# Zeroed rows in the recurrence, a weight split in pieces and a shared chunk: one change to a two-layer recurrent kernel with expert gates

## The reference

```
xn = layernorm(x)
s  = recurrence(xn)                  # layer 0
f  = experts(xn)                     # layer 0
x  = x + s * silu(f)
xn = layernorm(x)
s  = scan(xn)                        # layer 1: a two-component oscillator per state, 64 states
f  = ffn(xn)                         # layer 1: w2(silu(w1 xn) * (w3 xn)), inner width 704, 8 weight sets
x  = x + s * silu(f)
```

```
x_lerp = h + delta * x_proj_mu                      # delta = previous position - h
x0 = tanh(x_lerp @ xl_w1.T) @ xl_w2.T + xl_b2       # 256 -> 32 -> 160
x2 = einsum(tanh(x0) as 5 x 32, x_out_w)            # 5 x 256 blend weights
r, k, v, g = (h + delta * mu_i) @ W_i.T
w  = tanh((h + delta * w_mu) @ w_w1.T) @ w_w2.T + w_b          # 256 -> 64 -> 128
o_t = r_t . S + sum(r_t * bonus * k_t) * v_t ;  S = S * exp(-exp(w_t)) + k_t v_t
out = (groupnorm(o) * weight + bias) * silu(g) @ o_w.T
```

## Time and profile before

| what | us |
|---|---|
| median of the runs | 5183.19 |
| lowest, highest of 3 runs | 5174.28, 5184.97 |
| the profiled execution, its own time | 5169.71 |
| span in its trace | 5168.1 |

### The profile page before, as it was taken

One profiled execution on the slowest core, in us unless ns is written; L12 is line 12 of the kernel. 1 busy time (PEld: TensorE's weight loads), 2 busy tenths in 40 slices (PEclk: granted clock), 3 DMA queues, 4 the chain that ended last, 5 costly groups with the idle time before them and its releaser, 6 DMA issues. The chain is left out here.

```text
span 5168.1 us, 80399 instructions
## 1 busy us (share of the span) xinstructions
PE 4565.2 (88%) x29148; PEld 3603.7 (70%) x29148; DVE 2719.6 (53%) x5127; ACT 1988.2 (38%) x3685; POOL 1665.3 (32%) x1322
## 2 busy tenths in 40 slices
PE   6605999999999999799999999999997798888885
PEld 6604988988989899466666666666665677777774
DVE  4484333333333343365555555555554477777775
ACT  2203454444444444143333333333333343434431
POOL 1103444434344443332322222322332223333333
PEclk9999999999999999788887888888887899999998
DMA  6622322223232222100000000000000434433432
GB/s 207 219 94 66 50 53 57 44 57 59 39 63 41 60 42 36 32 21 17 22 17 22 17 18 21 22 17 17 21 17 16 132 83 99 97 91 89 99 66 37
DMA packets 246853, 294.07 MB, mean 57 GB/s; under 512 B 19041, under 2 KB 223585, under 8 KB 242401
## 3 DMA queue, kind: packets, MB, share of 16 engines
q0 software_dynamic: 85760, 117.74, 13.3%
q1 hardware_dynamic: 135136, 137.74, 8.3%
q10 hardware_dynamic: 25600, 33.56, 1.9%
HBM read 154.62 MB, written 134.35 MB: 56 GB/s over the span
## 5 line engine op out<-in xcount | busy, mean ns | idle before, releaser
L578 DVE TENSOR_TENSOR e_hTl<-e_hf,e_hTh 128x512 fp32r<-128x512 f32 x512 | 355.0, 694 | 775.0 <-ACT e_hTh L521 774.9
L1031 POOL TENSOR_TENSOR a_mix<-a_tmp,a_h 128x512 f32<-128x512 f32 x320 | 384.1, 1217 | 993.0 <-DVE a_tmp L1090 845.7
L442 POOL DMA_INDIRECT acc_d<-e_y,e_sids x256 | 402.4, 1572 | 723.8 <-DVE e_y L594 678.9
L520 ACT ACTIVATE e_hf<-ps_heads,e_b 128x512 f32<-128x512 f32 x512 | 353.2, 690 | 645.0 <-PE ps_heads L665 641.7
L665 PE MATMUL ps<-e_w2h,e_hTh 128*128 128x256 f32 x2048 | 585.7, 286 | 0.0
L665 PE MATMUL ps<-e_w2h,e_hTl 128*128 128x256 f32 x2048 | 583.6, 285 | 0.0
L665 PE MATMUL ps<-e_w2l,e_hTh 128*128 128x256 f32 x2048 | 577.7, 282 | 0.0
L665 PE MATMUL ps_heads<-e_xTh,e_w1h 128*128 128x512 f32 x1024 | 419.6, 410 | 41.6 <-ACT e_hTh L521 28.9
L665 PE MATMUL ps_heads<-e_xTh,e_w1l 128*128 128x512 f32 x1024 | 408.7, 399 | 0.0
L665 PE MATMUL ps_heads<-e_xTl,e_w1h 128*128 128x512 f32 x1024 | 407.7, 398 | 0.0
L665 PEld LDWEIGHTS ps<-e_w2h,e_hTh 128*128 128x128 f32 x2048 | 392.9, 192 | 19.8
(11 more groups left out here) (287 smaller groups left out, 10089.4 us busy)
## 6 DMA issues: line engine op xcount, KB each, us to landing
r_x<-in_L_attn_hidden_states SPq DMA_DIRECT2D x32, 512.0 KB, 3.8
xn_d<-r_xn ACTq DMA_DIRECT2D x32, 512.0 KB, 3.1
xnT_d<-r_xT ACTq DMA_DIRECT2D x32, 512.0 KB, 3.4
acc_d<-r_zeros POOLq DMA_DIRECT2D x16, 1024.0 KB, 21.1
e_w<-in_L_ffn_w SPq DMA_DIRECT2D x16, 1024.0 KB, 4.9
s_d<-a_s SPq DMA_DIRECT2D x32, 512.0 KB, 2.9
f_a<-acc_d SPq DMA_DIRECT2D x32, 512.0 KB, 3.8
f_x<-s_d SPq DMA_DIRECT2D x32, 512.0 KB, 5.2
```

Source lines behind the costliest of these rows:

```text
L442: pool.indirect_dma_start(acc_d, bass.IndirectOffsetOnAxis(ap=sids[:, GT * q + t:GT * q + t + 1], axis=0), ys[r][:, t, :], None, compute_o ...
L520: nc.scalar.activation(hf[m % 2][:], ps[2 + m % 2][:], ACT.Gelu, bias=b1s[:, m:m + 1])
L578: nc.vector.tensor_tensor(hT[q % 2][1][:, m, :], hf[m % 2][:], hT[q % 2][0][:, m, :].bitcast(F32), ALU.subtract).then_inc(h_sb, 1)
L1031: nc.gpsimd.tensor_tensor(mix[n][:, m, :].rearrange("p (c t) -> p c t", c=GT), tmp[i % 2][:].rearrange("p (c t) -> p c t", c=GT), h[q % 2] ...
```

## The change

It has three parts, one for each of the three large stages.

**Recurrence.** The six operands with few rows (`w2`, `xot`, `dw2`, `low`, `x1t`, `dlow`) become tiles of 128 rows and are set to zero by POOL once; loads and tanh outputs fill the rows in use, and the matmuls take all 128 rows. The zeroes add nothing to the sums. The count of matmuls and of their columns stays. The loads of the three weights move behind the zeroing. The fifth and sixth entry of `AT` move one piece later, and the r product with what hangs on it becomes a piece of its own, issued at the start of slot `CHUNK` (7) ahead of the chunk; `FRONT` grows from 7 to 8.

```
-        low = sb("a_low", [RANK, GN])
+        low = sb("a_low", [P, GN])
-        x1t = sb("a_x1t", [RANK, GN])
+        x1t = sb("a_x1t", [P, GN])
-        dlow = sb("a_dlow", [GATE, GN])
+        dlow = sb("a_dlow", [P, GN])
...
-        FRONT = SLOTS - LATE
+        FRONT = SLOTS - LATE + 1
-        AT = {2: (0, 1), 3: (2, 3), 4: (4, 5), 5: (6, 7), 6: (8, 9)}
+        AT = {2: (0, 1), 3: (2, 3), 4: (4, 5), 6: (6, 7), 7: (8, 9)}
...
-                        piece(g + 1, f1[1], s - LATE, False)
+                        piece(g + 1, f1[1], s - LATE if s < CHUNK else s - LATE + 1, False)
                 for s in range(SLOTS):
                     if s < LEVELS:
                         level(g, r, s, first)
+                    if left and s == CHUNK:
+                        piece(g + 1, f1[1], CHUNK - LATE, False)
...
-            nc.gpsimd.memset(xo[:], 0.0).then_inc(set_up, 1)
+            for operand in (xo, w2, xot, dw2, low, x1t, dlow):
+                nc.gpsimd.memset(operand[:], 0.0).then_inc(set_up, 1)
...
-                    nc.scalar.activation(low[:], ready(LOW)[0:RANK, :], ACT.Tanh).then_inc(act_out, 1)
+                    nc.scalar.activation(low[0:RANK, :], ready(LOW)[0:RANK, :], ACT.Tanh).then_inc(act_out, 1)
```

```
+        W2_PARTS = 4
+        W2_AT = {1: 0, 2: 1, 4: 2, 5: 3}
...
-            def split_down(e):
+            def split_down(e, n):
+                if n == 0:
+                    act.wait_ge(y_sum, YS * e + 1)
                 act.wait_ge(down_in, 32 * e + 32)
-                nc.scalar.copy(w2p[0][:], w2s[:]).then_inc(w2_high, 1)
+                nc.scalar.copy(w2p[0][:, w2_part(n), :], w2s[:, w2_part(n), :]).then_inc(w2_high, 1)
...
-                split_down(e)
+                nc.scalar.activation(table[:], ident[:, 0:1], ACT.Gelu)
...
+                        if q == 0 and m in W2_AT:
+                            split_down(e, W2_AT[m])
...
-                    act.wait_ge(down_ps, DOWNS * (e + 1))
```

```
-        w1s = sb("f_w1", [P, KD, FF])
-        w3s = sb("f_w3", [P, KD, FF])
+        w1s = sb("f_w1", [P, KD, FC * P])
+        w3s = sb("f_w3", [P, KD, FF - REST])
...
                 for m in range(FC):
                     multiply(g, m)
+                    scans = (j, r) if q == QB - 1 else (j - 1, 1 - r) if not first or k >= QB else None
+                    if scans:
+                        scan_part(*scans, q, m, 0, 1)
+                    low_h(g, m)
+                    if m == 2 and not last:
+                        statistics(i, k + 1)
                     if m == 3:
                         if not first or k >= LAG:
                             gated(g - LAG, (k - LAG) % PAIR)
                         if not last:
-                            statistics(i, k + 1)
-                    if m == 4 and not last:
-                        centre(g + 1)
-                    if q == QB - 1:
-                        scan_part(j, r, q, m)
-                    elif not first or k >= QB:
-                        scan_part(j - 1, 1 - r, q, m)
-                    low_h(g, m)
+                            centre(g + 1)
+                    if scans:
+                        scan_part(*scans, q, m, 1, None)
...
-                    if m == 5 and not last:
+                    if m == 4 and not last:
                         normalise(i, k + 1)
...
+                    if bank == 4 and m == FC - 1:
+                        break
                     if not begin or m >= 2:
                         pe.wait_ge(free, n - 1)
+                    if bank == 2 and not begin and m == (FC - 1) % 2:
+
+                        pe.wait_ge(h_sb, n - 1)
...
+                    else:
+                        for n, v in enumerate(w2p):
+                            done = nc.tensor.matmul(to, hT[0][:, m, u * P:(u + 1) * P], v[:, m, :], start=False,
+                                                    stop=n == 1 and u % 2 == 1)
```

More of the change, by code:

```diff
@@ L40 @@
 FC = (FF + P - 1) // P
-def width(m):
-    return min(P, FF - m * P)
+REST = FF - (FC - 1) * P
 class Order:
@@ L354, in experts_phase @@
         yl = sb("e_yl", [B, D])
+        table = sb("e_table", [P, 1])
         up_in = sem("e_up_in")
@@ L1641, in _ @@
             pool.sem_inc(down_split, 1)
-            for part in w1p + w3p + w2p:
-                nc.gpsimd.memset(part[:].bitcast(F32), 0.0).then_inc(padded, 1)
+            nc.gpsimd.memset(w2p[1][0:REST, FC - 1, :].bitcast(F32), 0.0).then_inc(padded, 1)
             nc.gpsimd.memset(power[:], -0.5).then_inc(set_up, 1)
```

161 lines of the change are left out of this document (94 added, 67 removed).

## The result

| | us |
|---|---|
| before, median of 4 runs | 5178.73 (5167.5 to 5184.97) |
| changed, median of 4 runs | 4757.05 (4751.61 to 4764.4) |
| ratio | 0.9191, 95% interval 0.9179 to 0.9203 |
| profiled execution, its own time and span | 4756.55 and 4755.0 |

The account below looks back on a forecast made before the run. PE was taken to bound all three stages, with its clock in the recurrence and clock and waits elsewhere. 290 + 69 + 115 = 474 us off 5169.7 gave 4696, stated as 4700, range 4625 to 4810.

Parts of the forecast that it names:

- the two slow stretches: Recurrence: per group 13.6 and 6.8 us at half clock; widening the operands ahead removes both, 28 x 10.2 = 286 us.
- The 6 us that were given to the earlier r product: Recurrence: moving the r product earlier saves 6 of the 19.1 us PE waits for the copy of r.
- Rival 2: Recurrence: rows have nothing to do with the clock; some 20 us instead of 290, total 4970; 8 in 100.
- Rival 1: Recurrence: only one slow stretch per group goes, or falls come back elsewhere; total 4795 or 4890; 9 in 100.
- Rival 4: Recurrence: r product, pulled ahead, blocks PE in order; 4880 one slot late, 5240 three slots late; 2 in 100.
- The step on the left-over matmuls: Experts: cutting the run of 48 16-column matmuls in four removes the half clock behind it, 24 us.
- 19.3 - 12.9 = 6.4 us, 7 times: 45 us: Experts: an expert's first group shrinks from 19.3 us to ACT's 12.9 us, at seven starts, 45 us.
- The light tiles: Second layer: removed matmuls and the vanished wait for normalised rows take these tiles from 30.8 to 27.4 us.
- the tiles with scans: Second layer: shorter waits for the low part take the two heavy tiles from 38.8 and 38.6 to 35.5 and 33 us.
- DVE is idle a quarter of the tile now, part of it while ACT casts the weights, and that stays: Second layer, tiles with scans: reason for taking 35.5 and 33 us, above DVE's limit of some 30 and 28.
- a bound from below of 59 us: Second layer: lowest gain expected, from the removed matmuls alone, 32 x 1.83 = 59 us.
- Rival 3: Second layer: DVE bounds tiles with scans, new order only moves waits; 59 us gain, total 4756; 11 in 100.

Follow-up runs that it names:

- the fastest kernel: Changed kernel plus later load of the experts' first weight and the second layer's up weights split in two parts at the old place: 4723.03 us, ratio 0.9116.

## Why the prediction was right, and where it was off

The time lies in the range, 57 us above the middle. The recurrence carries the result and was right in its mechanism; the two other stages gave less than was forecast, and the reasons were not among the rivals.

**The recurrence: right in mechanism, and in size by two errors that cancel.** 290 us were forecast, 298 came by the trace. Counting half of the two slow stretches was nearly the right price: 286 counted, 270 in the stage for the rows alone, since the jumps back of the loop now cost PE waits and short falls of the clock. The 6 us that were given to the earlier r product were too few: on top of the rows the new order gives 28 us in the stage, of which some 19 are the waits for the copy of r. Taken one by one the two pairs of few-row operands give 205 and 102 us, 190 and 95 by the same count.

The Trainium skill ("TensorE: Matmul & The Clock Gate", section "LDWEIGHTS (loading the stationary operand)") says that a weight's load time does not depend on its rows, and the traces agree: a load of `a_xot` takes 184 ns on the mean with 32 rows and 189 with 128. What its Part 1 says of the clock, that it is set by how busy PE has been, does not cover this case: the stretches at 0.50 are those in which PE is 100% busy.

Rival 2 is out. Rival 1 is out for the whole change, but falls that come and go without a change of rows are what the order alone and a_x1t alone show. Rival 4's block of PE never came. A new wait of over 1 us on PE did come, in one group of four.

**The experts were forecast at 69 and gave 40.** The step on the left-over matmuls held: 24 forecast, 27.5 found, and no fall behind them. The step that failed is the start of an expert, "19.3 - 12.9 = 6.4 us, 7 times: 45 us", in two terms. The first is the count. The eighth expert stands behind the loop, without a jump, and its first group took 13.3 us before the change already; the 28.9 us of waits are six of 4.4 to 4.9 us and one of 0.5, not seven. Six times 6.4 is 38 us. The second is the wait ahead of the start. ACT and the casts went as reckoned, but the sum began at PE's first matmul: the unnamed wait of 2.02 us in the earlier trace rows was taken as fixed. With PE sooner at the jump, the fetch of its instructions met the 1 MB load, the wait grew by 2.2 us on the mean, and half clock around it kept the first group at 15.2 us on the mean instead of 12.9. So 19.7 - 15.2 - 2.2 = 2.3 us are left of each start, 14 us for six. With the load out of the way the stage takes 1591.5 us, 64 less than before, which is what six starts and the left-over rows make in the forecast's own prices (38 + 24 = 62).

**The second layer was forecast at 115 and gave 80.** The light tiles came out as said (27.4 forecast, 27.2 found). For the tiles with scans 35.5 and 33 were forecast and in the group shown 32.4 and 38.7 came: the first gained twice what was reckoned, the second nothing. The step that failed there is "DVE is idle a quarter of the tile now, part of it while ACT casts the weights, and that stays". It stayed, and became PE's wait: the splits of w1 and w3, which PE reached late before, now bound the tile's head, and they take longer than before. In the changed kernel the two on DVE run beside one of POOL:

```profile
4062.40 2.20 DVE L1760 TENSOR_TENSOR f_w1l<-f_w,f_w1h 128x1536 fp32r<-128x1536 f32 x1 [0.87 <-ACT f_w3h L1952]
4064.53 2.55 DVE L1760 TENSOR_TENSOR f_w3l<-f_w,f_w3h 128x1280 fp32r<-128x1280 f32 x1
```

```profile
4061.70 4.03 POOL L1703 TENSOR_TENSOR f_xd<-f_xn,f_dv 128x512 f32<-128x512 f32 x2 [4.80 <-DMA out<-f_xd]
```

The kernel before took 1.62 us for each, with 1408 columns. What the two of now take with POOL quiet, an earlier tile of the same trace shows:

```profile
3818.06 1.75 DVE L1760 TENSOR_TENSOR f_w1l<-f_w,f_w1h 128x1536 fp32r<-128x1536 f32 x1
3819.73 1.49 DVE L1760 TENSOR_TENSOR f_w3l<-f_w,f_w3h 128x1280 fp32r<-128x1280 f32 x1
```

So 0.45 and 1.06 us come from running beside POOL, whose two additions take 4.03 us here and 2.56 a tile later. The Trainium skill ("GPSIMD Engine Reference", section 1, Specifications) lists the two engines' path to memory as shared, with contention when a DVE instruction has two inputs there; the trace agrees, 1.5 us on the path of PE. The second thing off was the base: the group of four tiles that was read takes 138.8 us, the mean of six groups 134.7 before and 124.6 after (from a tile's first up matmul to the next one's). The gain of 15.7 us a group came out as 10.1: 6.5 in the two light tiles, 6.8 being forecast, and 3.5 in the two heavy ones (73.9 to 70.4), 8.9 being forecast, which is no more than their removed matmuls are worth.

The third is not in the sum and matters most to a reader. The matmuls that each of 32 tiles loses, 1.83 us, made a bound from below of 59 us. Alone, that edit makes the kernel 31 us slower. That the stage stayed above this bound is owed to the new order in the same change, not to the reasoning of the bound.

**The sum.** 8 more in the recurrence, 29 less in the experts, 35 less in the second layer: 418 us where 474 were forecast, 56 us less, nearly the distance from 4700 to 4757. Rival 3's 4756 is the measured time to a microsecond, and that is an accident: it has 59 us in the second layer, where 80 came, and the full 69 in the experts, where 40 came. Of its mechanism, that DVE bounds the tiles with scans, something is true: in the fastest kernel DVE is busy 32.06 of the 34.90 us of such a tile.

## What to carry to other kernels

Before cutting work from a saturated engine, look at what it waits for next and whether the clock holds across that wait: matmuls that stand ahead of a late operand are cover, and taking them away can cost more than they did, so move the operand's producer first. Read the clock beside the busy share: for a stretch at half clock with a busy PE, look at the rows of the matmuls just ahead of it; widening those few to all rows with zeroes cost PE no time here. An edit that shifts a jump or a wait in time should be priced with the transfers that it will now lie beside, and the passes of a loop that have the wait should be counted one by one.

## What the runs showed of the hardware

- Matmuls of 512 columns last as long with 32 as with 128 rows (four in 1.98 us), yet some 2 us after the start of a run of the former, with other matmuls following without a pause, the granted clock was 0.50 for 6.8 to 13.6 us in most groups, and behind the latter it was not. With a_x1t alone widened, 8 of 31 groups had no fall behind the 32-row a_low either.
- Behind 48 matmuls of 16 columns in one run the clock fell to 0.50 for 6.8 us; with the same 48 in four runs of 12 between others it did not.
- The clock does also fall behind idle time: behind 3.2 us of wait in a light tile (0.90 over the tile), around 3.4 to 4.4 us at an expert's start (3.4 to 6.8 us at 0.50). Of six waits of 1.5 to 1.9 us at such starts, one was followed by a fall, of 3.4 us.
- A jump back to the loop's start costs PE 1.4 to 2.2 us with a quiet DMA and 3.4 to 4.4 us while a load of 1 MB, 4 us long, ends. PE starts again 1.6 to 2.0 us after a 16 KB packet of the kind "instruction" has ended, and that packet comes later when the load lies there.
- DVE with two operands and POOL beside each other: 2.55 us for 1280 columns against 1.49 alone, and 4.03 against 2.56 us for the same two POOL adds.
